# Vision-transformer tower on one core: second embedding piece and a bias line issued from ScalarE's queue

## What is computed

```
x = einsum('bchpwq,dcpq->bhwd', patches, conv_w).reshape(b, 256, 128) + conv_b
for i in range(2):
    y = layernorm(x) * ln1_g[i] + ln1_b[i]
    q, k, v = heads(y @ qkv_w[i]);  q = softmax(q, -1) / 8;  k = softmax(k, over tokens)
    x = x + (q @ (k^T v)) @ out_w[i] + out_b[i]
    x = x + gelu((layernorm(x) * ln2_g + ln2_b) @ ff1_w[i] + ff1_b[i]) @ ff2_w[i] + ff2_b[i]
h = (layernorm(x) * lnf_g + lnf_b) @ head_w + head_b
h = h + linear_attention(layernorm(h));  h = h + mixed_ffn(layernorm(h))
```

## Time and profile before

| what | value |
|---|---|
| median of three runs | 128.81 us (128.06 to 129.3) |
| the profiled execution's own time | 128.17 us |
| its span, first to last instruction of the program | 125.9 us |
| TensorE matmul busy in the span | 117.5 us, 93% |
| weight loads of TensorE | 101.5 us, 81% |
| VectorE, ScalarE, GpSimd busy | 76.9, 63.1, 45.8 us |

### The profile page before, as it was taken

The page is one execution under the profiler, slowest core; times in us unless marked ns, Lnnn a source line. Parts: engine busy times, 40 slices in busy tenths (PEclk is TensorE's granted clock), DMA queues, the critical chain, the costliest instruction groups (busy, mean ns, idle before and its releaser), DMA issues.

```text
span 125.9 us, 2263 instructions
## 1 busy us (share of the span) xinstructions
PE 117.5 (93%) x854; PEld 101.5 (81%) x854; DVE 76.9 (61%) x244; ACT 63.1 (50%) x152; POOL 45.8 (36%) x56
## 2 busy tenths in 40 slices
PE   6999999999999999998999899977989988999991
PEld 6988999985977888896856789966677877998990
DVE  5000364997686965779999897639498467155002
ACT  4001242845469387295774976444862635323520
POOL 0000024034799824205939759375213031041000
PEclk9999999999999999999999999999999999999999
DMA  4999999999400000000000000000000000000101
GB/s 103 367 414 427 376 412 323 416 427 371 107 0 0 0 3 5 0 0 0 0 0 5 0 0 0 3 5 0 0 0 0 0 0 5 0 0 0 62 0 62
DMA packets 3915, 12.26 MB, mean 97 GB/s; under 512 B 457, under 2 KB 1849, under 8 KB 3650
## 3 DMA queue, kind: packets, MB, share of 16 engines
q1 hardware_dynamic: 3906, 12.14, 25.6%
HBM read 11.74 MB, written 0.39 MB: 96 GB/s over the span
## 4 chain that ended last, share of the span: by engine, by line
PE 73%; DVE 12%; DMA 5%; ACT 4%; issue 2%; POOL 1%; SPq 1%; ACTq 0%
PE bank L326 10%; PE bank L419 6%; PE bank L524 6%; DMA embed_sb<-in_embed 5%; PE bank L438 5%; PE bank L395 4%; PE bank L412 3%; PE bank L390 3%; PE bank L360 3%; PE bank L372 2%; PE bank L426 2%; PE bank L510 2%; PE bank L348 2%; PE bank L404 2%; PE bank L517 2%
## 5 line engine op out<-in xcount | busy, mean ns | idle before, releaser
L1843 POOL TENSOR_TENSOR rstd<-mv,minus_half 128x2 f32<-128x2 f32 x14 | 10.0, 711 | 46.5 <-DVE mv L958 46.4
L1861 POOL TENSOR_TENSOR qn<-q,rqsum 128x512 f32<-128x512 f32 x8 | 8.4, 1046 | 10.9 <-DVE rqsum L1028 10.9
L1582 ACT ACTIVATE kexp<-bank,nkmax 128x256 f32<-128x256 f32 x16 | 7.5, 473 | 6.0 <-DVE nkmax L1008 6.0
L1624 ACT ACTIVATE patches_sb<-bank,fcb 128x256 f32<-128x256 f32 x12 | 5.1, 471 | 10.5 <-PE bank L521 10.5
L419 PEld LDWEIGHTS bank<-cw,qT 128*128 128x128 f32 x64 | 8.0, 191 | 2.4 <-issue 1.5
L419 PE MATMUL bank<-cw,qT 128*128 128x128 f32 x64 | 8.9, 280 | 0.7 <-DVE x L1043 0.4
L524 PE MATMUL bank<-projw,patches_sb 128*128 128x192 f32 x48 | 9.4, 331 | 0.0
L438 PE MATMUL bank<-restw,hid 128*128 128x128 f32 x64 | 8.8, 281 | 0.1
L1598 ACT ACTIVATE hid<-bank,small_sb 128x256 f32<-128x256 f32 x16 | 6.5, 473 | 3.6 <-PE bank L433 3.6
L438 PEld LDWEIGHTS bank<-restw,hid 128*128 128x128 f32 x64 | 7.8, 191 | 0.6 <-issue 0.3
L952 DVE BATCH_NORM_STATS2 stats<-bank 128x6 f32<-128x128 f32 x4 | 1.1, 272 | 11.7 <-PE bank L334 11.7
(11 more groups left out here) (172 smaller groups left out, 334.5 us busy)
## 6 DMA issues: line engine op xcount, KB each, us to landing
embed_sb<-in_embed SPq DMA_DIRECT2D x3, 768.0 KB, 7.1
patches_sb<-in_patches SPq DMA_DIRECT2D x2, 1024.0 KB, 12.1
restw<-in_rest_w SPq DMA_DIRECT2D x2, 768.0 KB, 15.4
qkvw<-in_qkv_w SPq DMA_DIRECT2D x3, 256.0 KB, 10.5
qkvw<-in_qkv_w SPq DMA_DIRECT2D x1, 768.0 KB, 15.4
fcw<-in_fc_w SPq DMA_DIRECT2D x1, 768.0 KB, 18.3
embed_sb<-in_embed SPq DMA_DIRECT2D x1, 576.0 KB, 3.9
aqkvw<-in_aqkv_w SPq DMA_DIRECT2D x1, 576.0 KB, 11.1
```

The costliest lines, as they stand in the source:

```text
L1582: return nc.scalar.activation(kexp[:, c, :], K_BANK[s][c // 2][:, (c % 2) * TOKENS:(c % 2 + 1) * TOKENS], ACT.Exp, bias=nkmax[i][:, c:c + ...
L1843: return nc.gpsimd.tensor_tensor(rstd[i][:], mv[i][:, :, 1], minus_half[:], ALU.pow)
L1861: return nc.gpsimd.tensor_tensor(qn[:, t, :].rearrange("p (h d) -> p h d", h=HEADS), q[:, t, :].rearrange("p (h d) -> p h d", h=HEADS), rq ...
```

## The change

Two loads are taken out of SyncE's list and put at the head of ScalarE's program, ahead of its first wait. SyncE's list becomes embed0, embed2, embed3, embed4, patches1a, and the rest as it was; ScalarE issues embed1 and then first_row. Tiles, semaphores, sizes and every consumer are as before.

```diff
             load_embed(0, 1, "embed0")
-            load_embed(1, 4, "embed1")
             load_embed(4, 8, "embed2")
-            load(first_row_sb, first_row, "first_row")
             load_embed(8, 12, "embed3")
             load_embed(12, 16, "embed4")
             load_patches(0, 8, "patches1a")
...
+            act.dma_start(embed_sb[:, 1:4, :], embed0[:, 1:4, :]).then_inc(loaded["embed1"], 16)
+            act.dma_start(first_row_sb, first_row).then_inc(loaded["first_row"], 16)
             act.wait_ge(first_rows_done, 1)
             evict(norm_rows_sb[0][:], FIRST_ROWS_BANK[:, 0:GROW]).then_inc(first_rows_ready, 1)
```

## The result

The changed kernel took 130.05 us, the median of four runs (129.72 to 130.88), beside 128.83 us for the kernel before: a ratio of 1.0135 on record, 95% interval 1.0096 to 1.0174. The two medians alone give 1.0095, just under that interval; by either it is slower. The forecast said 129.6 us, +0.6%, range 128.3 to 131.0, with 0.30 for slower by over 1%; the time lies in the range, above the forecast's own 129.2 to 129.9. The profiled execution took 130.05 us, its span 127.8 us against 125.9: +1.9 us. The profiled execution of the kernel before (128.17 us) was faster than its median, so the traces differ by 1.88 us where the medians differ by 1.22.

The account below looks back on a forecast made before the run. The kernel was taken to be bound by when TensorE begins chunk 4 (7.87 us). TensorE's start +0.8 us, all else 0: profiled 128.17 becomes 129.0, by the median 129.6 us (+0.6%); range 128.3 to 131.0.

Parts of the forecast that it names:

- what binds, and that nothing swallows a shift: Head of the path: TensorE's start of chunk 4 (7.87 us) decides; a microsecond before it is one of the whole.
- embed0 no longer moves alone: First loads: embed0 and embed1 share the engines by packets in turn, so embed0 lands at 4.85 us instead of 3.54.
- embed1 beside it: First loads: embed1 was to land together with embed0, at 4.85 us.
- The issues on ScalarE and first_row cost nothing: ScalarE's opening: two issues of 0.38 to 0.42 us each fit its idle time, first_row lands in time; cost 0.
- Embed1 comes late: ScalarE's opening: table load goes first, embed1 lands at about 7.3 us, chunk 4 at 9.4; loss 1.5 us; chance 0.15.
- TensorE's pace: Chunk 0 to chunk 4 on TensorE: the work stays 3.81 us, between a fast-pace 3.1 us and a longer slow pace.
- Its own sign of being wrong: Weight loads of 323 ns in chunks 1 to 3 would show the slow pace there, instead of the expected 192 ns.
- The slow pace lasts: TensorE's idle time keeps chunks 1 to 3 slow: chunk 4 at 10.2 us, loss 2.3 us, 131.1 us; chance 0.15.
- midway form: The pace rises partway through the slow stretch before chunk 4: loss some 1.6 us, 130.4 us; within the 0.15 chance.
- the two terms: Ahead of chunk 4: TensorE's late start, a loss of 0.8 us, and its pace, unchanged at 3.81 us of work.
- late start: TensorE idle about 0.8 us, chunk 0 at 4.9 us, chunk 4 at 8.7 against 7.87; loss about 0.8 us.
- lower branch: Fast pace at its old moment: chunk 0 to chunk 4 takes 3.1 us, chunk 4 at 8.0 to 8.1, loss 0.1 to 0.2.

Follow-up runs that it names:

- held kernel: The changed kernel with ScalarE waiting for embed0 to land before it issues embed1; ratio to the kernel before 1.0591 (1.0541 to 1.0641).
- lines exchanged: The changed kernel with first_row issued ahead of embed1 on ScalarE, embed1 0.43 us later; ratio to the kernel before 1.0218 (1.0126 to 1.0310).
- run with six warm-ups: The changed kernel with six opening warm-ups on TensorE instead of four; ratio to the kernel before 1.0024 (0.9991 to 1.0057).
- run with two warm-ups: The kernel before with two opening warm-ups on TensorE instead of four, loads unchanged; ratio to the kernel before 1.0037 (0.9998 to 1.0076).

## Why the prediction was right, and where not

**Right: what binds, and that nothing swallows a shift.** In the traces chunk 4 came 1.81 us late, the bias matmuls 1.87, the span 1.9.

**Right: embed0 no longer moves alone.** This step chose 4.85 us for a landing between 3.54 and 5.08, by packets in turn; it was 4.9. Chunk 0 was put at 4.9 and started at 4.97; embed2 at 7.6 landed at 7.6. Only "embed1 beside it" was off: embed1 landed at 5.5, which the warm-ups covered. The held kernel and the one with the lines exchanged, where embed0 lands at 3.4 and 3.2 us, show that embed1's packets were the cause.

**Right: the issues on ScalarE and first_row cost nothing.** The table load stands behind them, which takes away the condition of the rival *Embed1 comes late*. The experiment with the lines exchanged shows that rival's price, though by another way: 2.04 us idle ahead of chunk 1.

**Wrong in size: TensorE's pace.** The step said "I take the middle: the same 3.81 us, 0.8 late." It was 4.71 us. That term of the sum was mis-sized by 0.90 us, which is most of what the forecast of +0.8 us was short of the traces' 1.88; by the medians it was short by 0.4. Its own sign of being wrong, slow weight loads in chunks 1 to 3, showed in half of them (334 ns), and chunk 4 started at 9.68 and not near 8.7. What took its place is the rival *The slow pace lasts* in its midway form, "some 1.6 us, 130.4"; it had 0.15 in all. The step read the rise at 5.1 us as following some 4 us without idle time, from one trace; the other traces have it at 4.0 to 6.8 us with no idle time at all, so that reading did not hold. It also took the granted clock of 1.00 at the opening for the 2.4 GHz level, where the trace has no record of it; the held kernel has the same slow loads at 0.50. In the changed kernel's trace the rise lies at 8.5 us, after an idle time of 0.92 us (4.05 to 4.97). The run with six warm-ups shows that filling this idle time takes the loss away; the run with two warm-ups, 1.0037 (0.9998 to 1.0076), does not show the reverse. How much of the 0.90 us was the idle time and how much this one execution stays open, and that the time came out within the range owes something to that spread.

**Not seen: that the two terms are one.** The prediction gave the late start 0.8 us and the pace none on top. The run with six warm-ups shows that the start 1.1 us late costs nothing clear of noise when the fast pace comes early. The prediction had this as its lower branch (loss 0.1 to 0.2 us; measured 1.0024, 0.9991 to 1.0057); but it did not see that the warm-ups help to choose the branch, though their end at 4.05 us stood in its own rows.

## What to carry to other kernels

A second queue does not put a transfer ahead of another: issued together, two pieces shared the engines here, and a small piece that is needed first should not be issued beside a larger one on another queue. When TensorE opens on warm-ups, count whether they last until the first piece lands; an idle time there can be paid again in all that runs at the slow pace. Before reading a pace from one trace, look at how much its moment differs between executions. And compare the work after a late start with the hole it closes before calling it a loss: here 1.1 us late cost nothing clear of noise once the engine was kept busy.

## What was not expected of the hardware

A transfer that ScalarE issued at 3.46 us moved its first packet only between 6.5 and 7 us, after some 1.8 MB that SyncE had issued before, while of two transfers issued within 0.01 us of each other the second moved its first packets at 2.2 us, after 0.03 MB of the first. What sets how much goes ahead was not measured by itself.

TensorE's slow pace at the opening does not show in the view's granted clock, which reads 1.00 while weight loads take 334 ns; the records of that clock begin only at the rise, in each of the twelve traces. Later it does show: with TensorE idle from 5.7 to 11.3 us in the held kernel, the granted clock fell to 0.50 of full speed, the 1.2 GHz level, between 8 and 10 us, and the weight loads behind the idle time took 329 ns, as at the opening.
